# Two attentions with shared keys: a third bank for transposed score products, maxima turned on VectorE and sent through DRAM, values products at later steps

## The chip, the cores and the metric

The kernel runs on one core of one Trainium2 chip. The time is the device's, in microseconds (us), from the start to the end of one execution. Names: TensorE (PE; its weight loads PEld), VectorE (DVE), ScalarE (ACT), GpSimd (POOL), SyncE (SP, which issues DMAs here).

## The reference

A block of four layers on x of 4 x 512 x 512, each an attention and a feed-forward part. The change touches the attentions of layers 2 and 3, which compute the same thing (layer 3 names its arguments otherwise):

```python
def _L3_xattn_ref(q, k, v):
    QH, KVH = (32, 8)
    D = E // QH                      # 16
    G = QH // KVH                    # 4 query heads share one key head
    qh = q.reshape(b, s, KVH, G, D).transpose(0, 2, 3, 1, 4)
    kh = k.reshape(b, s, KVH, D).transpose(0, 2, 1, 3)
    vh = v.reshape(b, s, KVH, D).transpose(0, 2, 1, 3)
    scores = jnp.einsum('bkgsd,bktd->bkgst', qh, kh) * scale
    attn = jax.nn.softmax(scores, axis=-1)
    out = jnp.einsum('bkgst,bktd->bkgsd', attn, vh)
...
x = x + _L3_xattn_ref(_layernorm(x, axis=-1), ctx_512, ctx_512)
```

With a batch of 4 and 8 key heads there are 32 groups of four query heads in each layer, and 512 queries by 512 keys in each head.

## The kernel before

`stage_attend_shared` computes one such attention. Its unit of work is a *slot*: one group `s` of four heads (GROUPS is 32). Slots 1 to 24 are three turns of a loop over eight slots, the others are written out.

A group's scores are computed twice, in two forms. `scores` (L1529) puts queries on the partitions; 16 products of 128x512, two to a *set*. VectorE reduces each set to the maxima of its rows (`max_set`, L1648). Two buffers of two banks hold the sets (`score[m % 2]`), so the product of step 2m+4 waits until set m is reduced. `scores_T` (L1540) puts keys on the partitions, in 16 steps n (key tile n // 4, head n % 4), with the maximum already subtracted: the maxima of the group are two more rows of `qT` (high and low part), against rows of -1 in `kT`. ScalarE takes the exponential of each (L1628) into one of eight `probs`, and `results` (L1553, a round of four heads, after 4 of the 16 steps) multiplies them with the values into one bank `res`. The bank is copied out (`move_res`, L1620), turned on TensorE (`turn_results`, L1565), divided by its sum on VectorE (`finish`, L1663 and L1666) and added to x by GpSimd (L1701).

In slot s TensorE issues for each n the transposed product of group s and, right behind it, the plain product of group s + 2. The two read different halves of the partitions (`half(par, ...)`, bases 0 and 64, and the parities are opposite). After step LAST = 1 comes the last round of values products of the slot before, after steps 5, 9 and 13 (VALUES) the first three of this slot. After MAX = 5 comes `turn_max` (L1560): the split maxima of group s + 1 are turned by TensorE into bank 7, copied by ScalarE (`move_max`, L1615) and put into `qT` by four DMAs (`put_max`, L1495). After RES = 9 comes `turn_results` into the same bank 7. The transposed products alternate between two banks, 4 and 5, so that of step n waits for the exponential of step n - 2 (`exped`).

VectorE's slot has this order, which the change leaves as it is, and in which RES sets the place of `finish`:

```python
def slot(s, place, j, ahead):
    if ahead >= 1:
        split_maxima(s + 1, place + 1)
    for m in range(SETS):
        if ahead >= 2:
            max_set(s + 2, m)
        if m == (RES + 1) // 2 and not is_first(s):
            finish(s - 1)
```

SP loads group s + 3 in each slot (`load`, 12 DMAs, L1482 and L1485) and then puts the maxima of group s + 1. Before the first slot it also stores the queries' high and low parts to DRAM (`spill`, L1468), from which the loads read them.

Of the kernel before, what the change touches and what calls it, by code (L numbers as in the profile page):

```python
# [1384 lines left out]
def stage_attend_shared(k, nm, ctx_g, q_hi, q_lo, k_hi, k_lo, factor, queries):  # L1385
# [12 lines left out]
    LAST, VALUES, MAX, RES = 1, (5, 9, 13), 5, 9  # L1398
    with stage_room(k) as room:
        ctx, block = room.memory, room.block  # L1400

        def sb(name, shape, dt=F32):
# [14 lines left out]
        (cleared, consts, spilled, scored, maxed, max_split, turned_max, max_moved, scoredT, exped, valued, vals_kept, res_moved, turned_res,  # L1417
         inv_made, finished, added) = k.sems(
            ctx, nm, "cleared consts spilled scored maxed max_split turned_max max_moved scoredT exped valued vals_kept res_moved turned_res "
# [29 lines left out]

        @block.vector  # L1450
        def _(dve):
            for r in range(SLOTS):
                dve.memset(kT[r][:, :].bitcast(F32), -1.0).then_inc(cleared, 1)
            for r in range(2):
                dve.memset(vals[r][:, :, :], 0.0).then_inc(consts, 1)
                dve.memset(split[r][:, :, :, :].bitcast(F32), 0.0).then_inc(consts, 1)
            dve.wait_ge(consts, 4)
# [13 lines left out]
        def _(sp):  # L1471
# [15 lines left out]
            def put_max(place, j, g):  # L1487
# [15 lines left out]
            put_max(0, 0, 0)  # L1503
            sp.wait_ge(spilled, 2 * B * DMA)

            def slot(s, place, j, ahead):
                if ahead >= 3:
# [3 lines left out]
                if ahead >= 1:  # L1511
                    put_max(place + 1, j, s + 1)
# [4 lines left out]
        def _(pe):  # L1517
# [16 lines left out]
            def scores_T(g, place, j, n):  # L1534
# [4 lines left out]
                pe.wait_ge(exped, PAIRS * g + n + 1)  # L1539
                pe.matmul(scoreT[n % 2][:, :], kT[r][half(h % 2, USED + 2), t * P:(t + 1) * P], qT[r][half(h % 2, USED + 2), h // 2, :],  # L1540
# [15 lines left out]
            def turn_max(g, place):  # L1556

                pe.wait_ge(max_split, 2 * (g + 1))
# [1342 lines left out]
```

## Time and profile before

| | |
|---|---|
| median of 3 runs | 4062.18 us (4059.2 to 4066.68) |
| profiled execution, its time | 4080.94 us |
| its span | 4079.3 us |
| mean granted clock of TensorE | 0.91 of full |
| slots with all parts (1 to 29) | 29 in each of two layers |

The trace is of the one profiled execution. Durations and starts in it are in us from the span's start. A view gives for an instruction its start, its time, its engine and line, what it writes and reads, how many were merged (x4), and in brackets how long the engine was idle before it and which work released it. Matmuls overlap, so their times don't add up; their starts do. The granted clock is 1.00 at 2.4 GHz and 0.50 at 1.2 GHz.

### The profile page before, as it was taken

How to read it: one execution, taken by the hardware profiler on the slowest of the kernel's cores; microseconds unless marked ns; L12 is line 12 of the kernel's file. 1: busy time of each engine (PE TensorE's matmuls, PEld its weight loads, DVE VectorE, ACT ScalarE, POOL GpSimd, SP SyncE). 2: the span in 40 equal slices, each digit the busy share in tenths (PEclk: the TensorE clock that was granted, in tenths of full speed). 3: DMA queues.
4: the chain of work that ended last, by engine and by line, in shares of the span. 5: the costliest groups of instructions: out<-in, count | busy, mean ns of one | idle time of the engine just before them, and what ended most of it. 6: DMA issues, size and time to landing. Idle time of an engine off the chain costs nothing. (4 is left out here: it accounts for less than half of the span.)

```text
span 4079.3 us, 62234 instructions
## 1 busy us (share of the span) xinstructions
PE 3337.4 (82%) x17174; PEld 2276.6 (56%) x17174; DVE 2324.2 (57%) x3679; ACT 1934.3 (47%) x3331; POOL 606.2 (15%) x901
## 2 busy tenths in 40 slices
PE   3359996899871999668888689899897788878998
PEld 2137775666551788533332367888775233326886
DVE  6954445455443343477777444566567676745565
ACT  5643333355530555346666433566433566654333
POOL 2410001544223000210000030122111000000000
PEclk7669998999985999869999799999997999989999
DMA  3424442400011333341111152567443211102223
GB/s 137 147 98 139 139 138 89 165 0 0 11 52 62 111 119 107 111 152 43 42 41 32 70 183 93 193 242 240 167 141 119 71 40 41 42 21 67 96 94 113
DMA packets 174475, 404.47 MB, mean 99 GB/s; under 512 B 28484, under 2 KB 28612, under 8 KB 173682
## 3 DMA queue, kind: packets, MB, share of 16 engines
q1 hardware_dynamic: 141010, 286.47, 22.0%
q0 software_dynamic: 22480, 96.23, 6.9%
q10 hardware_dynamic: 10864, 20.45, 1.3%
q8 instruction: 41, 0.67, 0.1%
q14 instruction: 80, 0.66, 0.1%
HBM read 312.32 MB, written 87.03 MB: 98 GB/s over the span
## 5 line engine op out<-in xcount | busy, mean ns | idle before, releaser
L1648 DVE TENSOR_REDUCE at_maxima<-psum 128x2 f32<-128x1024 f32 x512 | 623.9, 1223 | 259.5 <-PE psum L1529 241.8
L1628 ACT ACTIVATE at_probs<-psum 128x512 f32<-128x512 f32 x1024 | 568.4, 595 | 368.0 <-PE psum L1540 337.6
L1540 PE MATMUL psum<-at_qT,at_kT 50*128 50x512 f32 x1024 | 452.1, 491 | 177.8 <-ACT at_probs L1628 167.7
L1540 PEld LDWEIGHTS psum<-at_qT,at_kT 50*128 50x128 f32 x1024 | 175.9, 192 | 496.9 <-ACT at_probs L1628 438.6
L1529 PE MATMUL psum<-at_kT,at_qT 48*128 48x512 f32 x1024 | 431.4, 496 | 14.6 <-DVE at_maxima L1648 12.4
L573 PE MATMUL psum<-f_xT_hi,ffn_w_hi 128*128 x1024 | 406.8, 397 | 9.9 <-DVE f_xT_lo L313 2.8
L573 PE MATMUL psum<-f_xT_lo,ffn_w_hi 128*128 x1024 | 405.9, 396 | 0.0
L1553 PE MATMUL psum<-at_probs,at_vals 128*32 128x512 f32 x2048 | 292.7, 640 | 0.0
L590 PE MATMUL psum<-ffn_w_hi,ffn_hid_hi 128*128 128x512 f32 x768 | 269.3, 391 | 1.3 <-ACT ffn_hid_hi L636 1.3
L387 PE MATMUL psum<-ident,n_normed 128*128 128x128 f32 x448 | 95.5, 389 | 195.9 <-ACT n_normed L353 159.3
L478 ACT ACTIVATE ffn_w_hi<-ffn_w_raw 128x512 fp32r<-128x512 f32 x262 | 161.6, 633 | 157.3 <-PE psum L595 100.1
L573 PEld LDWEIGHTS psum<-f_xT_hi,ffn_w_hi 128*128 128x128 f32 x1024 | 194.0, 189 | 56.7 <-issue 12.1
L486 DVE TENSOR_TENSOR ffn_w_lo<-ffn_w_raw,ffn_w_hi 128x512 fp32r<-128x512 f32 x262 | 176.7, 686 | 76.1 <-ACT ffn_w_hi L478 75.9
L573 PEld LDWEIGHTS psum<-f_xT_lo,ffn_w_hi 128*128 128x128 f32 x1024 | 193.9, 189 | 44.5
L595 PE MATMUL psum<-ffn_w_hi,ffn_hid_lo 128*128 128x512 f32 x768 | 205.3, 389 | 0.0
L1325 DVE TENSOR_REDUCE at_maxima<-psum 128x1 f32<-128x128 f32 (+3 forms) x256 | 122.5, 489 | 141.9 <-PE psum L1135 138.3
L573 PE MATMUL psum<-f_xT_hi,ffn_w_lo 128*128 x512 | 202.5, 396 | 0.0
L592 PE MATMUL psum<-ffn_w_lo,ffn_hid_hi 128*128 128x512 f32 x512 | 199.5, 390 | 0.0
L387 PEld LDWEIGHTS psum<-ident,n_normed 128*128 128x128 f32 x448 | 79.8, 204 | 212.0 <-issue 147.8
L1529 PEld LDWEIGHTS psum<-at_kT,at_qT 48*128 48x128 f32 x1024 | 170.8, 194 | 28.5 <-DVE at_maxima L1648 22.7
L676 DVE TENSOR_TENSOR n_normed<-n_normed,psum 128x512 f32<-128x512 f32 (+1 forms) x88 | 60.4, 687 | 217.2 <-ACT n_normed L633 211.0
L1296 ACT ACTIVATE at_probs<-psum 128x512 f32<-128x512 f32 (+3 forms) x256 | 111.9, 438 | 136.9 <-PE psum L1149 136.7
(399 smaller groups left out, 7354.9 us busy)
## 6 DMA issues: line engine op xcount, KB each, us to landing
ffn_w_raw<-in_stream SPq DMA_DIRECT2D x262, 256.0 KB, 2.7
ffn_w_hi<-quantized SPq DMA_DIRECT2D x66, 512.0 KB, 3.5
ffn_w_hi<-quantized SPq DMA_DIRECT2D x65, 256.0 KB
at_qT<-q_hi SPq DMA_DIRECT2D x256, 64.0 KB, 2.2
ffn2a_w_raw<-in_shared2a SPq DMA_DIRECT2D x26, 512.0 KB
ffn2b_w_raw<-in_shared2b SPq DMA_DIRECT2D x26, 512.0 KB
qz_raw<-in_stream SPq DMA_DIRECT2D x17, 768.0 KB, 4.2
quantized<-qz_quant POOLq DMA_DIRECT2D x16, 768.0 KB, 3.5
```

What stands on the lines that cost most here:

```text
L387: mm = pe.transpose(turned_ps[u][:, c, :], normed[u][:, c * P:(c + 1) * P], k.ident[:, :])
L478: act.activation(hi[slot][:, :], raw[slot][:, :], ACT.Copy).then_inc(made, 1)
L486: dve.tensor_tensor(lo[slot][:, :], raw[slot][:, :], hi[slot][:, :].bitcast(F32), ALU.subtract).then_inc(made, 1)
L573: mm = pe.matmul(hid_ps[h][s][0:n, :], wt[s][:, w], xt[:, c, bass.ds(b * S, S)], start=(c == 0 and i == 0), stop=(c == DC - 1 and i == len ...
L590: pe.matmul(out[t][:, :], hid_hi[s][0:n, tok], w2_hi[s][0:n, :], start=first, stop=False)
L592: pe.matmul(out[t][:, :], hid_hi[s][0:n, tok], w2_lo[s][0:n, :], start=False, stop=False)
L595: mm = pe.matmul(out[t][:, :], hid_lo[s][0:n, t * P:(t + 1) * P], w2_hi[s][0:n, :], start=False, stop=last)
L1529: mm = pe.matmul(score[m % 2][:, 512 * (n % 2):512 * (n % 2) + S], qT[r][half(par, USED), jj, t * P:(t + 1) * P], kT[r][half(par, USED), : ...
L1540: pe.matmul(scoreT[n % 2][:, :], kT[r][half(h % 2, USED + 2), t * P:(t + 1) * P], qT[r][half(h % 2, USED + 2), h // 2, :], start=True, sto ...
L1553: pe.matmul(res[h * OW:(h + 1) * OW, :], vals[place % 2][:, t, :], probs[n % RING][:, :], start=(t == 0), stop=(t == TB - 1), tile_positio ...
L1628: act.activation(probs[n % RING][:, :], scoreT[n % 2][:, :], ACT.Exp, scale=factor).then_inc(exped, 1)
L1648: dve.tensor_reduce(maxima[:, t, 2 * jj:2 * jj + 2], score[m % 2].rearrange("p (h s) -> p h s", h=2), AX.X, ALU.max).then_inc(maxed, 1)
```

## The change

1. Transposed score products rotate through three banks, 4 to 6 (`turn_of`); the results' bank moves to 7. The turned results no longer have a bank of their own: they take the place of one product in the rotation, after step RES, now 7. The transposed product of step n waits for the exponential of step n - 3 where the rotation allows, and that of step 10 waits for `finish` of the slot.
2. The maxima are no longer turned by TensorE and copied by ScalarE. VectorE splits them into a 128x32 tile, turns it by blocks of 32x32 (`across`), and SP sends that tile to a DRAM buffer `tops` (`send_max`, ahead of the loads) and reads it back into `qT` with four DMAs (`put_max`, behind the loads), whose pieces are 32 elements long.
3. LAST is 2 and VALUES are 6, 10, 14; `move_res` still follows the exponential of step 2.

`turn_max`, `move_max` and their waits go. `finish` keeps its rule, `m == (RES + 1) // 2`, so it follows set 4 where it followed set 5.

```diff
-    LAST, VALUES, MAX, RES = 1, (5, 9, 13), 5, 9
+    LAST, VALUES, MOVE, RES = 2, (6, 10, 14), 2, 7
+    TURNS = 3
...
-        maxima, inv = sb("maxima", [P, TB, H]), sb("inv", [P, TB, H])
-        split = [sb(f"split{r}", [P, TB, P // 2, 2], F32R) for r in range(2)]
-        maxT = [sb(f"maxT{r}", [2 * H, S]) for r in range(2)]
+        maxima, inv = sb("maxima", [P, H, TB]), sb("inv", [P, TB, H])
+        split = sb("split", [P, H, 2, TB], F32R)
+        across = [sb(f"across{r}", [P, 2 * H * TB]) for r in range(2)]
         result = sb("result", [P, TB, H * HD])
-        score, scoreT, res, turn = [room.psum[:, 1024 * m:1024 * m + 1024] for m in range(2)], room.banks[4:6], room.banks[6], room.tiles(7)
+        score, scoreT, res = [room.psum[:, 1024 * m:1024 * m + 1024] for m in range(2)], room.banks[4:4 + TURNS], room.banks[7]
+        turn = room.tiles(4 + (RES + 1) % TURNS)
...
+        def turn_of(n):
+
+            return (n if n <= RES else n + 1) % TURNS
...
+            def send_max(place, g):
+
+                sp.wait_ge(max_turned, g + 1)
+                sp.dma_start(tops[place % SLOTS, :, :], across[place % 2][:, :]).then_inc(max_out, DMA)
+
+            def put_max(place, g):
 
                 r = place % SLOTS
-                sp.wait_ge(max_moved, g + 1)
+                sp.wait_ge(max_out, DMA * (g + 1))
+                rows = tops[r, :, :].rearrange("(b h o t) i -> h o t b i", b=TB, h=H, o=2)
                 for jj in range(2):
                     for par in range(2):
                         at = HALF * par + USED
-                        row0 = 2 * (2 * jj + 1 - par)
-                        sp.dma_start(qT[r][at:at + 2, jj, :].bitcast(F32), maxT[place % 2][row0:row0 + 2, :]).then_inc(put[r], DMA)
+                        dst = qT[r][at:at + 2, jj, :].bitcast(F32).rearrange("o (t b i) -> o t b i", t=TB, b=TB)
+                        sp.dma_start(dst, rows[2 * jj + 1 - par]).then_inc(put[r], DMA)
 
             spill(sp, 0)
             sp.wait_ge(spilled, 2 * DMA)
@@ -1500,16 +1511,19 @@
                 load(g, 0)
             for b in range(1, B):
                 spill(sp, b)
-            put_max(0, 0, 0)
+            send_max(0, 0)
+            put_max(0, 0)
             sp.wait_ge(spilled, 2 * B * DMA)
 
             def slot(s, place, j, ahead):
+                if ahead >= 1:
+                    send_max(place + 1, s + 1)
                 if ahead >= 3:
                     if not is_first(s):
                         sp.wait_ge(scoredT, PAIRS * s)
                     load(place + 3, j)
                 if ahead >= 1:
-                    put_max(place + 1, j, s + 1)
+                    put_max(place + 1, s + 1)
...
-                pe.wait_ge(exped, PAIRS * g + n + 1)
-                pe.matmul(scoreT[n % 2][:, :], kT[r][half(h % 2, USED + 2), t * P:(t + 1) * P], qT[r][half(h % 2, USED + 2), h // 2, :],
+                if n < 2:
+                    pe.wait_ge(exped, PAIRS * g + n + 1)
+                elif n > 2:
+                    pe.wait_ge(exped, PAIRS * g + (n + 1 if RES < n < RES + TURNS else n))
+                if n == RES + TURNS and not is_first(g):
+                    pe.wait_ge(finished, g + 1)
+                pe.matmul(scoreT[turn_of(n)][:, :], kT[r][half(h % 2, USED + 2), t * P:(t + 1) * P], qT[r][half(h % 2, USED + 2), h // 2, :],
...
-            def turn_max(g, place):
-
-                pe.wait_ge(max_split, 2 * (g + 1))
-                for t in range(TB):
-                    mm = pe.transpose(turn[:, t, :], split[place % 2][:, t, :, :].rearrange("p c o -> p (c o)").bitcast(F32), k.ident[:, :])
-                mm.then_inc(turned_max, 1)
-
...
-                    if n == MAX and ahead >= 1:
-                        pe.wait_ge(max_moved, s + 1)
-                        if not first:
-                            pe.wait_ge(finished, s)
-                        turn_max(s + 1, place + 1)
                     if n == RES and not first:
                         pe.wait_ge(res_moved, s)
-                        if ahead >= 1:
-                            pe.wait_ge(max_moved, s + 2)
-                        else:
-                            pe.wait_ge(finished, s)
+                        pe.wait_ge(exped, PAIRS * s + n + 1)
                         turn_results()
 
             all_slots(pe, slot)
             results(GROUPS - 1, GROUPS - 1, TB - 1)
             pe.wait_ge(res_moved, GROUPS)
-            pe.wait_ge(finished, GROUPS)
             turn_results()
 
...
-            def move_max(g, place, j):
-
-                act.wait_ge(turned_max, g + 1)
-                if not (isinstance(g, int) and g < 2):
-                    act.wait_ge(put[(place + 2) % SLOTS], PUTS * DMA * (use(place - 2, j) + 1))
-                act.activation(maxT[place % 2][:, :], turn[0:2 * H, :, :].rearrange("p t q -> p (t q)"), ACT.Copy).then_inc(max_moved, 1)
...
-                    act.activation(probs[n % RING][:, :], scoreT[n % 2][:, :], ACT.Exp, scale=factor).then_inc(exped, 1)
-                    if n == LAST + 1 and not is_first(s):
+                    act.activation(probs[n % RING][:, :], scoreT[turn_of(n)][:, :], ACT.Exp, scale=factor).then_inc(exped, 1)
+                    if n == MOVE and not is_first(s):
                         move_res(s - 1)
-                    if n == MAX + 1 and ahead >= 1:
-                        move_max(s + 1, place + 1, j)
...
-                dve.tensor_reduce(maxima[:, t, 2 * jj:2 * jj + 2], score[m % 2].rearrange("p (h s) -> p h s", h=2), AX.X, ALU.max).then_inc(maxed, 1)
+                dve.tensor_reduce(maxima[:, 2 * jj:2 * jj + 2, t], score[m % 2].rearrange("p (h s) -> p h s", h=2), AX.X, ALU.max).then_inc(maxed, 1)
...
             def split_maxima(g, place):
-                hi, lo = split[place % 2][:, :, 0:H, 0], split[place % 2][:, :, 0:H, 1]
+                hi, lo = split[:, :, 0, :], split[:, :, 1, :]
                 dve.wait_ge(maxed, 2 + SETS * (g + 1))
-                if not (isinstance(g, int) and g < 2):
-                    dve.wait_ge(turned_max, g - 1)
+                if not (isinstance(g, int) and g < 1):
+                    dve.wait_ge(max_turned, g)
                 dve.tensor_copy(hi, maxima[:, :, :]).then_inc(max_split, 1)
                 dve.wait_ge(max_split, 2 * g + 1)
                 dve.tensor_tensor(lo, maxima[:, :, :], hi.bitcast(F32), ALU.subtract).then_inc(max_split, 1)
                 dve.wait_ge(max_split, 2 * g + 2)
+                if not (isinstance(g, int) and g < 2):
+                    dve.wait_ge(max_out, DMA * (g - 1))
+                dve.transpose(across[place % 2][:, :], split[:, :, :, :].rearrange("p h o t -> p (h o t)").bitcast(F32)).then_inc(max_turned, 1)
 
```

## Rows read from the trace of the kernel before

**Rows 1.** The page, busy us (share of the span) and instructions

```profile
PE 3337.4 (82%) x17174; PEld 2276.6 (56%) x17174; DVE 2324.2 (57%) x3679; ACT 1934.3 (47%) x3331; POOL 606.2 (15%) x901
```

**Rows 2.** Busy time by stretch, the last two slots of each stage

```profile
core 0: us, PE busy (x) PEld busy (x) DVE busy (x) ACT busy (x) POOL busy (x), PEclk, DMA share, GB/s
...
2240.12:2276.50 36.38, 29.99 (x120) 9.55 (x120) 2.48 (x7) 19.81 (x37) 1.68 (x3) 0.77 0.00 1
...
3618.30:3659.50 41.20, 34.61 (x120) 10.73 (x120) 2.88 (x9) 19.85 (x37) 1.68 (x3) 0.63 0.00 1
```

**Rows 3.** The same view, one slot (from split to split) a line

```profile
3215.39:3229.91 14.52, 11.96 (x74) 4.47 (x72) 10.65 (x13) 9.64 (x19) 0.97 (x2) 1.00 0.18 42
...
3456.55:3472.63 16.08, 13.51 (x74) 5.00 (x72) 10.64 (x13) 9.62 (x19) 0.96 (x2) 0.89 0.14 39
```

**Rows 4.** Timeline of TensorE in one slot: start, us, line, work, count [idle before <-releaser]

```profile
3218.59 0.50 PE L1540 MATMUL psum<-at_qT,at_kT 50*128 50x512 f32 x1 [0.40 <-ACT at_probs L1628]
...
3219.02 1.07 PE L1553 MATMUL psum<-at_probs,at_vals 128*32 128x512 f32 x8
...
3220.01 0.66 PE L1560 MATMUL psum<-ident,at_split 128*128 128x128 f32 x4
...
3220.60 0.50 PE L1540 MATMUL psum<-at_qT,at_kT 50*128 50x512 f32 x1
...
3220.60 0.72 PE L1529 MATMUL psum<-at_kT,at_qT 48*128 48x512 f32 x2
...
3220.94 0.39 PE L1540 MATMUL psum<-at_qT,at_kT 50*128 50x512 f32 x1
...
3221.78 0.49 PE L1540 MATMUL psum<-at_qT,at_kT 50*128 50x512 f32 x1 [0.46 <-ACT at_probs L1628]
```

**Rows 5.** Timeline of ScalarE and of VectorE in the same slot

```profile
3216.96 0.60 ACT L1628 ACTIVATE at_probs<-psum 128x512 f32<-128x512 f32 x1 [0.83 <-PE psum L1540]
...
3221.13 0.60 ACT L1628 ACTIVATE at_probs<-psum 128x512 f32<-128x512 f32 x1 [1.41 <-PE psum L1540]
...
3221.63 0.57 ACT L1615 ACTIVATE at_maxT<-psum 8x512 f32<-8x512 f32 x1
...
3215.60 0.18 DVE L1657 TENSOR_TENSOR at_split<-at_maxima,at_split 128x16 fp32r<-128x16 f32 x1
...
3219.16 1.22 DVE L1648 TENSOR_REDUCE at_maxima<-psum 128x2 f32<-128x1024 f32 x1 [0.70 <-PE psum L1529]
...
3225.55 1.23 DVE L1648 TENSOR_REDUCE at_maxima<-psum 128x2 f32<-128x1024 f32 x1 [1.02 <-PE psum L1529]
...
3226.69 0.25 DVE L1663 RECIPROCAL at_inv<-psum 128x16 f32<-128x16 f32 x1
...
3226.97 0.42 DVE L1666 TENSOR_TENSOR at_result<-psum,at_inv 128x256 f32<-128x256 f32 x1
```

**Rows 6.** Timeline of all engines, start of the second stage

```profile
3142.97 9.13 DVE L1648 TENSOR_REDUCE at_maxima<-psum 128x2 f32<-128x1024 f32 x8
...
3144.24 0.79 PE L1529 MATMUL psum<-at_kT,at_qT 48*128 48x512 f32 x2 [1.30 <-DVE at_maxima L1648]
```

**Rows 7.** SP's timeline in that slot, L1482 to landing, the second stage's first T

```profile
3214.25 0.34 SPq L1482 DMA_DIRECT2D at_qT<-q_hi  x1
...
3219.43 0.37 SPq L1485 DMA_DIRECT2D at_kT<-k_lo  x1
...
3222.22 2.44 SPq L1495 DMA_DIRECT2D at_qT<-at_maxT  x4
...
DMA to landing us min/median/max: 2.1/2.3/4.0
...
3170.56 0.79 PE L1540 MATMUL psum<-at_qT,at_kT 50*128 50x512 f32 x1 [9.78 <-DMA at_qT<-at_maxT]
```

**Rows 8.** Timeline of TensorE about one fall of the granted clock

```profile
3461.17 0.66 PE L1560 MATMUL psum<-ident,at_split 128*128 128x128 f32 x4
...
3463.88 0.49 PE L1540 MATMUL psum<-at_qT,at_kT 50*128 50x512 f32 x1 [0.37 <-ACT at_probs L1628]
...
3464.30 1.91 PE L1553 MATMUL psum<-at_probs,at_vals 128*32 128x512 f32 x8
```

More of the change, by code:

```diff
@@ L1382, in _, with stage_attend_shared @@
             finish(groups - 1)
-def stage_attend_shared(k, nm, ctx_g, q_hi, q_lo, k_hi, k_lo, factor, queries):
+def stage_attend_shared(k, nm, ctx_g, q_hi, q_lo, k_hi, k_lo, tops, factor, queries):
     HD, H, PARTS = HEAD2, 4, 3
@@ L1455, in _ @@
                 dve.memset(vals[r][:, :, :], 0.0).then_inc(consts, 1)
-                dve.memset(split[r][:, :, :, :].bitcast(F32), 0.0).then_inc(consts, 1)
-            dve.wait_ge(consts, 4)
+            dve.wait_ge(consts, 2)
             for r in range(2):
@@ L1485, in load @@
                         sp.dma_start(kT[r][at:at + HD, :].bitcast(F32), src[n * HD:(n + 1) * HD, tokens]).then_inc(landed[r], DMA)
-            def put_max(place, j, g):
+            def send_max(place, g):
+                sp.wait_ge(max_turned, g + 1)
+                sp.dma_start(tops[place % SLOTS, :, :], across[place % 2][:, :]).then_inc(max_out, DMA)
+            def put_max(place, g):
                 r = place % SLOTS
-                sp.wait_ge(max_moved, g + 1)
+                sp.wait_ge(max_out, DMA * (g + 1))
+                rows = tops[r, :, :].rearrange("(b h o t) i -> h o t b i", b=TB, h=H, o=2)
                 for jj in range(2):
@@ L1566, in turn_results @@
                 mm.then_inc(turned_res, 1)
-            pe.wait_ge(consts, 6)
+            pe.wait_ge(consts, 4)
             for g in range(2):
@@ L1571, in _ @@
                     scores(g, g, 0, n)
-                    if g == 1 and n == MAX:
+                    if g == 1 and n == 0:
                         pe.wait_ge(made, before + N // P)
-                        turn_max(0, 0)
             def slot(s, place, j, ahead):
@@ L1620, in move_res @@
                 act.activation(resT[:, :], res[:, :], ACT.Copy).then_inc(res_moved, 1)
-            move_max(0, 0, 0)
             def slot(s, place, j, ahead):
@@ L1642, in _ @@
             dve.sem_inc(finished, 1)
-            dve.wait_ge(consts, 6)
+            dve.wait_ge(consts, 4)
             def max_set(g, m):
@@ L1701, in add @@
                 pool.tensor_tensor(xt, xt, result[:, :, :], ALU.add).then_inc(added, 1)
-            pool.wait_ge(consts, 6)
+            pool.wait_ge(consts, 4)
             keep_values(0, 0)
@@ L2672, in build_program @@
         ("quantized", (D * 4 // P + 2, P, 3 * D)), ("gathered1", (N, D)), ("answers1", (N + 1, D)),
-        ("q_hi", (D, N)), ("q_lo", (D, N)), ("k_hi", (P, N)), ("k_lo", (P, N)), ("gathered2", ((BLOCKS2 + 1) * BLOCK2, D)), ("answers2", (BLOCKS2 * BLOCK2, D)))}
+        ("q_hi", (D, N)), ("q_lo", (D, N)), ("k_hi", (P, N)), ("k_lo", (P, N)), ("tops", (4, P, 32)), ("gathered2", ((BLOCKS2 + 1) * BLOCK2, D)), ("answers2", (BLOCKS2 * BLOCK2, D)))}
     with ExitStack() as program:
@@ L2777, in build_program @@
                 stage_attend_shared(k, f"at{layer}", ctx_g, scratch["q_hi"], scratch["q_lo"], scratch["k_hi"], scratch["k_lo"],
-                                    1.0 / np.sqrt(HEAD2), queries)
+                                    scratch["tops"], 1.0 / np.sqrt(HEAD2), queries)
                 with ExitStack() as q_ctx:
```

4 lines of the change are left out of this document (2 added, 2 removed).

## Prediction

> **What bounds the kernel now.** The page comes first: TensorE is busy in 82% of the span [rows 1], so a first thought would be that only its own work counts. The change touches only the two shared-key attentions, which end at 2276.5 and 3659.5 us [rows 2]. The view of busy time by stretch cuts them from one splitting of maxima to the next, which is one slot (one group of four heads). An undisturbed slot takes 14.51 or 14.52 us, and 49 of the 58 full slots lie within 0.11 us of that; two per layer hold a loop's jump, and five are about 1.5 us longer at a granted clock of 0.89 [rows 3]. In a slot TensorE is busy 11.96 us, VectorE 10.65, ScalarE 9.64: none is full, so what counts is who waits for whom.
>
> The timeline of one slot shows that [rows 4, 5]. I write T(n) for the transposed score product of step n (L1540), S(n) for the plain one (L1529), E(n) for its exponential, R(m) for the reduction of S(2m) and S(2m+1), V for a round of values products. T(n) and S(n) start together, and use different halves of the array's rows (bases 0 and 64, exchanged by parity). A V holds the engine 1.00 us (3219.02 to the turning at 3220.01), a turning 0.59 us; a lone pair holds it 0.43 us before a V may start (3218.59 to 3219.02), and a second pair starts 0.34 us after the first (3220.60, 3220.94) [rows 4]. ScalarE starts E 0.53 us after its T (3220.60 to 3221.13), its operations follow each other by 0.49, and the T that needs the bank starts 0.65 us after E started (3221.13 to 3221.78) [rows 4, 5]. With two banks for T that loop is what paces the slot: after each V ScalarE stood idle 0.83 us, after V and a turning 1.41 [rows 5]. VectorE is behind nobody: it starts R 0.57 us after a lone pair (3218.59 to 3219.16) or 0.46 after a second one, and every V stands behind an odd n, when the pair of products of a reduction is complete, so that R runs under the V.
>
> **The change, part by part.** All in us per slot, for a slot at full clock, counted from T(15) of the slot before, which now follows a V.
>
> *Removed:* the turning of maxima on TensorE (0.59) and the copy of maxT on ScalarE (0.57) [rows 4, 5]. ScalarE has slack, so only the first could matter.
>
> *Third bank:* T(n) needs E(n-3) and no longer E(n-2), save at n = 0, 1, 8, 9. It removes ScalarE's idle time behind each V. That is a real gain if nothing else waits.
>
> *Later V:* V now follows n = 2, 6, 10, 14, even steps, between S(2m) and S(2m+1). The reduction of that set can start only behind the V. S(2m+4) needs it (two score buffers), and S(2m+4) stands ahead of the next V in TensorE's order. So a stretch from V to V costs: 0.57 (S to the start of R), 1.27 from the start of R to the product that needs its buffer (3142.97 to 3144.24, the start of both stages, where VectorE paces) [rows 6], 0.43 for the last pair, 1.00 for V: **3.27**. TensorE's own work there is 1.00 + 0.43 + 3 x 0.23 = 2.12. (0.23: two pairs end 0.72 to 0.73 after their start, one 0.50 [rows 4].)
>
> *Turned results in the ring:* the turning now stands behind n = 7 and takes a ring bank, so T(10) waits for VectorE's finish of that slot. But VectorE's slot still has finish behind R(4), at (RES+1)//2 = 4, and R(4) needs S(9). That puts on TensorE's path what was hidden: S(9), R(4), reciprocal, multiplication, T(10). From row to row: R to reciprocal 1.14, to multiplication 0.28, its 0.42, 0.05 to the product: 1.89 (3225.55, 3226.69, 3226.97) [rows 5].
>
> The slot, worked through: T(15) 0; S(15) lets R(7) start at 0.57; S(2) waits for it, 0.57 + 1.27 = 1.84; V 2.27 to 3.27; S(3) 3.27, R(1) 3.84, S(6) 5.11, V 5.54 to 6.54; S(7) 6.54; turning 6.97 to 7.56; T(8) 7.56, T(9) 7.90; R(4) 7.90 + 0.46 = 8.36; T(10) 8.36 + 1.89 = 10.25; V 10.68 to 11.68; S(11) 11.68, R(5) 12.25, S(14) 13.52, V 13.95 to **14.95**. I checked that E never is late in it: the latest, E(3) behind the move of the results, starts at 3.87 and T(6) may start at 4.52, before S(6). So 14.95 for 14.51, **+0.44** a slot, though all the exponentials' waits are gone. The same rules give 14.51 for the old order (12 of its starts come out within 0.02), which is why I trust them to 0.3 (four latencies to 0.07 each). Over 2 x 29 slots that have all parts: **+25** (8 to 43).
>
> *VectorE's transpose* of 128x32: no row shows one. It stands between R(7) and R(0). Bound below by the 0.18 of the split's 128x16, above by the 0.42 of a 128x256 operation [rows 5]; I take 0.2. R(0) then starts at 2.53 and R(1) could at 3.67, before its 3.84: hidden up to 0.17 more; at the upper bound 0.05 a slot, 3 in all.
>
> *Maxima through DRAM:* one more DMA ahead of the 12 loads in SP's queue (each 0.37, about 0.47 apart, 3214.25 to 3219.80), then four puts in 2.44 and 2.3 to land [rows 7]. Split at 2.0, sent at about 2.5 to 3.0, loads to 8.6, puts to 11.05, landed 13.3; T(0) of the next slot is at 15.3. Hidden by 2.0. At the start of each stage it is not: the first T waits for the puts already (3170.56; 9.8 us of idle time), and now a send lands first, 2.3 + 0.4, behind the spills: I take 4 a layer, **+8** (4 to 12).
>
> *Tail:* slots 30 and 31 have no S, and take 36.4 and 41.2 us, much of it at half clock, TensorE busy 30.0 and 34.6 [rows 2]. There the third bank helps: 6.5 of idle time to about 2.5, a turning less: 5 a layer, **-10** (-14 to 0).
>
> *The clock.* The five falls inside ordinary slots came about the end of a stretch between V's that holds a turning and four pairs: in one of them a V had ended at 3461.17, TensorE then had two waits for ScalarE, the last of 0.37, and the next V, at 3464.30, took 1.91 for its 1.07 [rows 4, 8]. The gap without a V was 3.13. Each fall cost 1.4 to 1.6 (16.08 for 14.52 the longest) [rows 3]. In the changed slot V to V there is 4.14 long (6.54 to 10.68), one pair less, and TensorE idle for 2 us at T(10). With the shorter gap the clock fell in 5 of 58 slots; with a longer one and less work in it I expect it much more often. I take a fall in 7 of 10 slots (bounds: 5 of 58, and all), at 1.1 each, since part of the slow time falls on waiting (bounds 0.9 and 1.45): 58 x 0.7 x 1.1 = 45, less the 7 of before: **+38** (0 to 77). The Trainium skill ("TensorE: Matmul & The Clock Gate", part 1, on the clock gate) says that the half clock is the default and that activity releases it; by that rule the removed turning and the wait both speak against this change. The falls in this trace agree, as far as they go.
>
> **Sum:** 25 + 8 - 10 + 38 = +61. The profiled execution took 4080.9 (span 4079.3), so its like would take 4142; it lies 18.8 above the median of 4062.2. Against the median: **4123**.
>
> **Rivals.**
> *A, no more falls of the clock:* the order is as worked out, TensorE's wait costs no clock. For it: 53 of 58 slots hold their clock with a gap of 3.1 between V's. Against it: the new gap is a third longer. +23, so 4085. Chance 0.14.
> *B, faster:* finish is not on the path. If T(10) didn't wait beyond R(3) (7.11 + 1.27 = 8.38), the slot would be four stretches of 3.27 = 13.08, -1.43, 58 x -1.43 - 2 = -85: 3977. For it: ScalarE's idle waits of 0.83 and 1.41 do vanish. Against it: VectorE's order and rows 5. It decides only if the 1.89 chain came to under 1.4 a slot in all; at 1.45 the gain is zero. Chance 0.09.
> *C, the terms cancel:* latencies at their low ends (+8), no falls: within 8 us of before. Chance 0.07.
> *D, maxima late:* the puts read 128-byte pieces from DRAM. If they took three times their 2.44, they would land at 18.2, 2.9 behind T(0): 58 x 2.9 = 168 more than A: 4253. It bites from 4.4 of puts. For it: nothing in the rows. Chance 0.05. The Trainium skill ("DMA: Bandwidth & Descriptors", why small descriptors are slow) holds small pieces in HBM to be slow; the transfers here are too few bytes for bandwidth to decide, and no row shows their time.
> The forecast itself has 0.65.
>
> **The range.** Its own: 61 with the clock term from 10 to 77 and the slot term from 8 to 43 gives 4085 to 4165. To leave out no more than 2 in 10 I reach down over A and up a little: 4075 to 4172. A change of under 0.2% (8 us) can't be told from none here. Faster: B, 0.09. Same: C and a little of A, 0.08. Slower: 0.83.
>
> **What will show it.** Slots of about 14.95 at a granted clock of 1.00 and of 16 at about 0.9, most of them the latter; TensorE idle some 2 us in front of T(10), released by VectorE's multiplication; S(6) and S(14) released by R; no waits of 0.83 on ScalarE; POOL and SP free; the four puts landed before T(0). Wrong would make it: T(10) starting right behind T(9), S starts that don't wait for R, or a clock at 1.00 in slots of 14.95 (then A).

## The result and the profile after

The changed kernel took 4303.82 us (median of 4 runs, 4292.57 to 4315.3), the kernel before on the same chip 4060.69 us (4053.97 to 4066.68): a ratio of 1.0599, with a 95% interval of 1.0562 to 1.0637. The direction was forecast; the size was not. The time lies 181 us above the predicted 4123 and 132 us above the end of the range.

The profiled execution took 4315.3 us with a span of 4312.5, at a mean granted clock of 0.834 (before: 4080.9, 4079.3, 0.91). The page of the changed kernel, its line of busy times and the three largest groups:

```profile
PE 3586.3 (83%) x16914; PEld 2348.5 (54%) x16918; DVE 2323.3 (54%) x3739; ACT 1901.2 (44%) x3267; POOL 607.8 (14%) x901
...
L1639 DVE TENSOR_REDUCE at_maxima<-psum 128x2 f32<-128x1024 f32 x512 | 612.1, 1220 | 500.5 <-PE psum L1543 499.4
...
L1559 PE MATMUL psum<-at_qT,at_kT 50*128 50x512 f32 x1024 | 530.9, 621 | 167.2 <-DVE at_result L1660 120.3
...
L1572 PE MATMUL psum<-at_probs,at_vals 128*32 128x512 f32 x2048 | 414.6, 892 | 0.0
```

TensorE issues 260 instructions fewer than before and is busy 249 us more [rows 1]. That cannot be work; the same products became longer (T takes 621 ns in the mean, where the page of before has 491). And there is a new releaser of T (now L1559): VectorE's finish multiplication (L1660), with 120.3 us of idle time.

Busy time by stretch tells where. The first two lines are the 29 slots of each stage that have all parts (from the split of slot 2 to that of slot 31), the other two the slot that is followed below and the last full one:

```profile
core 0: us, PE busy (x) PEld busy (x) DVE busy (x) ACT busy (x) POOL busy (x), PEclk, DMA share, GB/s
1814.14:2363.15 549.01, 473.99 (x1973) 169.46 (x1970) 309.26 (x377) 264.97 (x493) 28.04 (x58) 0.68 0.13 32
3299.97:3852.84 552.87, 479.60 (x1973) 170.42 (x1970) 309.28 (x377) 264.88 (x493) 28.06 (x58) 0.68 0.13 32
2213.35:2230.32 16.97, 14.50 (x69) 5.50 (x68) 10.67 (x13) 8.96 (x17) 0.97 (x2) 0.79 0.14 37
3831.00:3852.84 21.84, 19.52 (x69) 6.50 (x66) 10.64 (x13) 9.20 (x17) 0.96 (x2) 0.50 0.01 2
```

The same 29 slots took 430.98 and 432.67 us before, at granted clocks of 0.98 and 0.97. They grew by 118.0 and 120.2, 238.2 together. A slot takes 18.93 and 19.06 us in the mean, from 16.8 (clock 0.80) to 21.95 (0.50); before, 14.52 at 1.00 and 16.08 at 0.89 [rows 3]. Not one of the 58 ran at the full clock throughout. VectorE's work per slot is as it was (10.67 for 10.65), ScalarE's is less, as the copy of the maxima is gone (8.96 for 9.64).

The rest of the difference: the first two slots of each stage grew by 4.7 and 5.5 (from the first split to the third: 25.17 and 34.32 before, 29.86 and 39.84 after); the last ones (from the last full split to the last copy of results) took 34.28 and 38.62 and take 36.29 and 36.30, so nothing in sum. In the starts, the stage's first T waited 3.58 us for the puts in the first stage, where it did not wait before, and 13.55 in the second, where it was 9.78 [rows 7]:

```profile
3281.92 0.79 PE L1559 MATMUL psum<-at_qT,at_kT 50*128 50x512 f32 x1 [13.55 <-DMA at_qT<-tops]
```

The stages are 248.1 us longer, the span 233.2: between the two stages, where no line was changed, this execution took 860.7 us and that of before 876.9.

TensorE's timeline of one slot of the changed kernel shows the new order (T(15) of the slot before at 2211.51). This slot began at the full clock:

```profile
2211.51 0.50 PE L1559 MATMUL psum<-at_qT,at_kT 50*128 50x512 f32 x1
...
2213.79 1.07 PE L1572 MATMUL psum<-at_probs,at_vals 128*32 128x512 f32 x8
...
2216.64 0.49 PE L1543 MATMUL psum<-at_kT,at_qT 48*128 48x512 f32 x1
2217.06 1.06 PE L1572 MATMUL psum<-at_probs,at_vals 128*32 128x512 f32 x8
...
2218.48 0.66 PE L1577 MATMUL psum<-ident,at_resT 128*128 128x128 f32 x4
...
2221.87 0.47 PE L1559 MATMUL psum<-at_qT,at_kT 50*128 50x512 f32 x1 [2.06 <-DVE at_result L1660]
2221.98 0.49 PE L1543 MATMUL psum<-at_kT,at_qT 48*128 48x512 f32 x1
2222.40 1.13 PE L1572 MATMUL psum<-at_probs,at_vals 128*32 128x512 f32 x8
...
2226.33 1.94 PE L1572 MATMUL psum<-at_probs,at_vals 128*32 128x512 f32 x8
...
2231.06 1.93 PE L1572 MATMUL psum<-at_probs,at_vals 128*32 128x512 f32 x8
...
2242.71 0.76 PE L1559 MATMUL psum<-at_qT,at_kT 50*128 50x512 f32 x1 [2.07 <-DVE at_result L1660]
...
2247.98 1.07 PE L1572 MATMUL psum<-at_probs,at_vals 128*32 128x512 f32 x8
```

Read the column of starts: from V to V 3.27 us, then, over the turning and the wait, 5.34. T(10) starts 10.36 after T(15), after 2.06 of idle time, released by the finish. The very next V is the last short one; then V's take 1.94 and stand 4.73 apart, until 2247.98. Between this T(10) and the pause in front of the next one TensorE stands idle 0.26 us in all. The granted clock in the same stretch, by 1 us:

```profile
2221.00:2222.00 1.00, 0.13 (x2) 0.16 (x2) 0.69 (x3) 0.00 (x0) 0.09 (x1) 1.00 0.13 36
2222.00:2223.00 1.00, 1.00 (x10) 0.31 (x10) 0.00 (x0) 0.60 (x1) 0.64 (x1) 1.00 0.03 5
2223.00:2224.00 1.00, 1.00 (x10) 0.50 (x4) 0.00 (x0) 0.00 (x0) 0.00 (x0) 0.64 0.05 8
...
2246.00:2247.00 1.00, 1.00 (x7) 0.45 (x3) 0.73 (x1) 0.76 (x2) 0.00 (x0) 0.50 0.00 0
2247.00:2248.00 1.00, 0.95 (x8) 0.38 (x6) 1.00 (x2) 1.00 (x3) 0.00 (x0) 0.92 0.00 0
```

The clock falls 1.4 us after the wait has ended, while the engine works again, to its lower level (0.50 of the granted clock is 1.2 GHz, 1.00 is 2.4), and stays there for 24 us, past the next slot's wait.

The trace's record of the granted clock can be counted over the 58 slots. A fall is the start of a stretch at half clock (a low stretch) in one of them; the mean length counts each to its end:

| | falls | half clock within the slots, us | mean length of a low stretch, us |
|---|---|---|---|
| before | 9 | 44 | 4.9 (3.4 to 10.2) |
| after | 41 | 703 | 18.8 (3.4 to 65) |

The two of 65 us begin in the last full slot of the first stage and the last but one of the second, and run on through the last slots; the other 39 have a mean of 16.5, the longest 37.6. All 41 begin 0.1 to 1.7 us after the finish of a slot has ended; T(10) starts 0.15 after it. The clock was full at the end of the finish in exactly these 41 slots, and in the other 17 it was already low: where the wait met a full clock, the clock was lost every time. The engine comes back either 3.9 to 4.6 us after a finish (24 times) or about 18 us after one, just ahead of the next wait (14 times).

VectorE's timeline of that slot, with the split, the new transpose and the chain to T(10):

```profile
2213.35 0.18 DVE L1646 CAST at_split<-at_maxima 128x16 fp32r<-128x16 f32 x1
...
2213.86 0.21 DVE L1652 STREAM_TRANSPOSE at_across<-at_split 128x32 f32<-128x32 f32 x1
2214.00 1.20 DVE L1639 TENSOR_REDUCE at_maxima<-psum 128x2 f32<-128x1024 f32 x1
...
2218.62 2.48 DVE L1639 TENSOR_REDUCE at_maxima<-psum 128x2 f32<-128x1024 f32 x2 [0.91 <-PE psum L1543]
2221.01 0.25 DVE L1657 RECIPROCAL at_inv<-psum 128x16 f32<-128x16 f32 x1
2221.30 0.42 DVE L1660 TENSOR_TENSOR at_result<-psum,at_inv 128x256 f32<-128x256 f32 x1
```

The two reductions from 2218.62 are R(3) and R(4). Only after R(4), in the order that RES sets, come the reciprocal and the multiplication, whose end at 2221.72 lets T(10) go.

SP's queue, in two lines of its timeline, the send of maxima to DRAM and the four puts:

```profile
2214.10 0.35 SPq L1495 DMA_DIRECT2D tops<-at_across  x1
...
2220.49 2.54 SPq L1506 DMA_DIRECT2D at_qT<-tops  x4
```

The four puts of 128-byte pieces are issued in 2.54 us, against 2.44 before [rows 7], and no T(0) waits for them in the full slots.

### The profile page after: what moved, and what is told of

Its sections match the earlier page's. It is cut to its first block and busy times, and to the rows that moved or that the text cites. A ratio compares the mean times of both kernels' runs of the same rounds, so it can differ in the third digit from the quotient of the medians.

```text
span 4312.5 us, 61624 instructions
## 1 busy us (share of the span) xinstructions
PE 3586.3 (83%) x16914; PEld 2348.5 (54%) x16918; DVE 2323.3 (54%) x3739; ACT 1901.2 (44%) x3267; POOL 607.8 (14%) x901
## 5 line engine op out<-in xcount | busy, mean ns | idle before, releaser
L1639 DVE TENSOR_REDUCE at_maxima<-psum 128x2 f32<-128x1024 f32 x512 | 612.1, 1220 | 500.5 <-PE psum L1543 499.4
L1621 ACT ACTIVATE at_probs<-psum 128x512 f32<-128x512 f32 x1024 | 549.3, 599 | 608.6 <-PE psum L1559 603.4
L1559 PE MATMUL psum<-at_qT,at_kT 50*128 50x512 f32 x1024 | 530.9, 621 | 167.2 <-DVE at_result L1660 120.3
L1559 PEld LDWEIGHTS psum<-at_qT,at_kT 50*128 50x128 f32 x1024 | 234.2, 262 | 675.7 <-issue 399.6
L1543 PE MATMUL psum<-at_kT,at_qT 48*128 48x512 f32 x1024 | 549.6, 635 | 18.4 <-DVE at_maxima L1639 14.7
L1572 PE MATMUL psum<-at_probs,at_vals 128*32 128x512 f32 x2048 | 414.6, 892 | 0.0
L573 PE MATMUL psum<-f_xT_hi,ffn_w_hi 128*128 x1024 | 405.8, 396 | 10.2 <-DVE ffn_w_lo L486 2.6
L1543 PEld LDWEIGHTS psum<-at_kT,at_qT 48*128 48x128 f32 x1024 | 231.1, 259 | 94.8 <-DVE at_maxima L1639 89.4
```

Source lines behind the costliest of these rows:

```text
L573: mm = pe.matmul(hid_ps[h][s][0:n, :], wt[s][:, w], xt[:, c, bass.ds(b * S, S)], start=(c == 0 and i == 0), stop=(c == DC - 1 and i == len ...
L1543: mm = pe.matmul(score[m % 2][:, 512 * (n % 2):512 * (n % 2) + S], qT[r][half(par, USED), jj, t * P:(t + 1) * P], kT[r][half(par, USED), : ...
L1559: pe.matmul(scoreT[turn_of(n)][:, :], kT[r][half(h % 2, USED + 2), t * P:(t + 1) * P], qT[r][half(h % 2, USED + 2), h // 2, :], start=True ...
L1572: pe.matmul(res[h * OW:(h + 1) * OW, :], vals[place % 2][:, t, :], probs[n % RING][:, :], start=(t == 0), stop=(t == TB - 1), tile_positio ...
L1621: act.activation(probs[n % RING][:, :], scoreT[turn_of(n)][:, :], ACT.Exp, scale=factor).then_inc(exped, 1)
L1639: dve.tensor_reduce(maxima[:, 2 * jj:2 * jj + 2, t], score[m % 2].rearrange("p (h s) -> p h s", h=2), AX.X, ALU.max).then_inc(maxed, 1)
```

## The experiments

Each kernel was timed against the kernel before on the same chip, and the kernel before took from 4060.69 to 4087.94 us in these comparisons, so ratios are compared and not times. "V" and the letters are those of the prediction.

| | V after steps | finish after | ratio to before (95%) | slot at full clock, us (worked out) | clock of the two stages |
|---|---|---|---|---|---|
| the change | 2, 6, 10, 14 | R(4) | 1.0599 (1.0562 to 1.0637) | none (14.95) | 0.68, 0.68 |
| filled wait | 2, 6, 10, 14 | R(4) | 1.0056 (1.0017 to 1.0095) | 15.02 (14.95) | 1.00, 0.93 |
| odd steps | 1, 5, 9, 13 | R(4) | 0.9815 (0.9795 to 0.9834) | 13.10 (13.0) | 0.95, 0.93 |
| early finish | 2, 6, 10, 14 | R(3) | 0.9890 (0.9859 to 0.9921) | 13.90 (13.7) | 0.96, 0.94 |
| both | 1, 5, 9, 13 | R(3) | 0.9576 (0.9552 to 0.9599) | 11.99 (12.0) | 0.99, 1.00 |

### The wait filled with products

If it is the pause in front of T(10) that costs the clock, work put into the pause must give it back; if the change's order or its memory traffic made the products long, more work can only add.

```diff
-    scores_T(s, place, j, n)
-    if ahead >= 2:
-        scores(s + 2, place + 2, j, n)
+    if n == RES + TURNS and not first and ahead >= 2:
+        for _ in range(9):
+            scores(s + 2, place + 2, j, n)
+        scores_T(s, place, j, n)
+    else:
+        scores_T(s, place, j, n)
+        if ahead >= 2:
+            scores(s + 2, place + 2, j, n)
```

S(10) is computed nine times instead of once, and ahead of T(10).

> The changed kernel, with step 10 of each full slot in another order: the plain product S(10) is issued nine times into its own buffer (start=True each time, so the value is the same) ahead of T(10), which waits for VectorE's finish. This adds eight products of 0.23 us each to the 2.06 us in which TensorE stood idle, and nothing to the path. Theory clock (the order itself costs 0.6 us a slot, all else is the granted clock, which falls because TensorE stands idle here): the granted clock stays at 1.00 in most slots, a slot takes 15.0 to 15.3 us, the whole kernel about 4061 + 58 x 0.6 + 7 = 4103 us, within 4090 to 4130. Theory order (the even places of V and the wait for finish cost the 4.1 us a slot themselves, the lower clock is only a consequence of more waiting that costs little): no faster than the changed kernel, 4300 or more, since work is added.

4104.2 us against 4086.64. The 29 slots of the two stages, by stretch, and TensorE's timeline about one T(10):

```profile
1812.38:2250.87 438.49, 405.48 (x2206) 172.91 (x2210) 309.36 (x378) 262.76 (x494) 28.05 (x58) 1.00 0.16 41
3194.03:3654.25 460.22, 429.32 (x2209) 181.62 (x2210) 309.36 (x378) 263.34 (x494) 28.05 (x58) 0.93 0.15 39
```

```profile
3401.44 2.83 PE L1543 MATMUL psum<-at_kT,at_qT 48*128 48x512 f32 x10
3403.90 0.47 PE L1559 MATMUL psum<-at_qT,at_kT 50*128 50x512 f32 x1
3404.30 1.06 PE L1572 MATMUL psum<-at_probs,at_vals 128*32 128x512 f32 x8
```

Some 235 products were added to each stage, and the ratio to the kernel before fell from 1.0599 to 1.0056, which is over 200 us. The pause is gone (2.83 us of products stand there), T(10) starts when it did, and the slot takes 15.02 at a granted clock of 1.00. The second stage has 0.93 because its first three full slots (22.73, 22.81 and 19.49 us) ran in a low stretch that had begun before them, 102 us long. Four falls are left. This shows both the cause of the low clock and, undisturbed, the cost of the change's order: 0.50 us a slot.

### Values products at odd steps, finish after R(3), and both

```diff
-    LAST, VALUES, MOVE, RES = 2, (6, 10, 14), 2, 7
+    LAST, VALUES, MOVE, RES = 1, (5, 9, 13), 2, 7
```

> The changed kernel with LAST = 1 and VALUES = 5, 9, 13 as before, so that a V stands behind a complete pair of products; the third bank, the maxima through DRAM and the wait for finish at T(10) stay. Theory clock: the reduction runs under the V again, V to V takes 2.1 to 2.6 us at most, the idle time before T(10) is 1.0 us and lies under no gap between V's as long as 4.1; the clock holds; worked out by the same rules a slot takes 13.0 us; 58 x -1.5 from before's 4061 and +7 at the starts: about 3980 us (3950 to 4030). Rival (the wait for finish alone brings the clock down, whatever the places of V): idle time before T(10) remains, clock about 0.7 in the stage, slots of 17 or more, 4180 us or more.

```diff
-                    if m == (RES + 1) // 2 and not is_first(s):
+                    if m == (RES - 1) // 2 and not is_first(s):
```

> The changed kernel with finish placed behind R(3) instead of R(4) in VectorE's order; the even places of V stay. Worked out by the same rules T(10) starts at 9.0 instead of 10.25 and a slot takes 13.7 us at full clock. Theory clock: the gap between V's falls from 4.1 to 2.9 us and the idle time from 2.06 to 0.9, the clock falls in some slots only: slots of 13.7 to 16, total 4020 to 4150. Rival (even places of V keep the clock down by themselves, by VectorE's pace): mean granted clock in the stage stays near 0.68 and the total above 4200.

> Both edits: V at odd steps 1, 5, 9, 13 and finish behind R(3). By the same rules T(10) no longer waits for finish (8.9 against 9.33) and a slot takes 12.0 us, close to the 10.9 us that VectorE needs; the clock holds. 58 x -2.5 + 7: about 3923 us (3900 to 3980), faster than before. Rival (the maxima's way through DRAM is too slow for a shorter slot: split at 2.0, sent 0.5 behind it, loads to 8.6, puts to 11.1, landed 13.4): T(0) of the next slot then waits for the puts, a slot takes about 12.9 us and the total is about 3975 with T(0) released by a DMA.

They took 4010.8, 4045.77 and 3914.32 us against 4086.64. The first stage of odd steps with a T(10) of its second stage, the first stage of early finish and the second of both:

```profile
1810.55:2206.64 396.09, 347.11 (x1972) 131.12 (x1970) 309.07 (x377) 259.76 (x494) 28.16 (x58) 0.95 0.17 45
```

```profile
3201.67 0.47 PE L1559 MATMUL psum<-at_qT,at_kT 50*128 50x512 f32 x1 [1.07 <-DVE at_result L1660]
```

```profile
1813.42:2229.41 415.99, 364.43 (x1977) 134.16 (x1978) 306.82 (x377) 263.27 (x494) 28.13 (x58) 0.96 0.17 43
```

```profile
3112.30:3464.99 352.69, 333.87 (x1972) 127.89 (x1970) 306.58 (x377) 259.87 (x494) 28.12 (x58) 1.00 0.20 50
```

Either edit turns the loss into a gain. With odd steps a V runs between R(4)'s products and T(10), and the idle time there is 1.07 instead of 2.06; 13 low stretches begin, 133 us in all. With the early finish the chain no longer holds R(4), and T(10) waits 0.80: 6 low stretches, 68 us. With both, TensorE is busy 333.87 of 352.69 us, one low stretch of 6.8 us begins, and the kernel is 172 us faster than the one before. The rival stated for it came true in small: in 13 of its 58 full slots T(0) waited 0.5 to 1.4 us for the puts out of DRAM, 10.9 us in all, so the maxima's way has no slack left in slots of 12 us. The count of products is within five in all three and in the change; only the order differs.

### The parts of the change alone

To see whether a part of the change is a loss by itself, two kernels. First the kernel before with the later values products alone:

```diff
-    LAST, VALUES, MAX, RES = 1, (5, 9, 13), 5, 9
+    LAST, VALUES, MAX, RES = 2, (6, 10, 14), 5, 9
```

> The kernel before with LAST = 2 and VALUES = 6, 10, 14 alone: two banks, maxima turned on TensorE, the copy of the results behind E(3). By the rules of the prediction V to V takes 3.27 where no turning lies between and 3.63 with one, 13.8 us a slot against 14.5, and the longest gap without a V is 2.6 us. Theory: later V's alone are no loss while finish is off TensorE's path; no falls of the clock, about 4061 - 58 x 0.7 = 4020 (4000 to 4060, against this call's run of before by its ratio 0.985 to 1.0). Rival (the even places bring the clock down by themselves): more than 4150, granted clock under 0.85 in the stage.

4063.96 us against 4087.94: 0.9942 (0.9921 to 0.9964), 13.83 a slot at the full clock (13.80 worked out). Then the changed kernel with the maxima's way through VectorE and DRAM kept and the rest as before (two banks for T, results in bank 6 and turned in bank 7 behind step 9, with the wait for the finish back ahead of that turning, V at odd steps):

```diff
-    LAST, VALUES, MOVE, RES = 2, (6, 10, 14), 2, 7
-    TURNS = 3
+    LAST, VALUES, MOVE, RES = 1, (5, 9, 13), 2, 9
+    TURNS = 2
...
-        turn = room.tiles(4 + (RES + 1) % TURNS)
+        turn = room.tiles(7)
...
-                if n == RES + TURNS and not is_first(g):
-                    pe.wait_ge(finished, g + 1)
```

> The kernel before with the maxima's new way alone: split, transposed on VectorE, sent to DRAM and read back; two banks, the turned results in a bank of their own behind n = 9, V at 5, 9, 13. The turning (0.59) goes, and E(7) no longer stands behind the copy of the maxima, so T(9) starts 0.45 earlier: 13.5 us a slot against 14.5. With +3.4 at each stage's start: 4061 - 58 x 1.0 + 7 = 4010 (3990 to 4050; ratio 0.982 to 0.995). Rival (the puts come late through DRAM): T(0) waits for a DMA in each slot, 4060 or more.

4032.28 us against 4087.94: 0.9862 (0.9826 to 0.9897), 13.46 a slot (13.5 worked out). The first stage of each:

```profile
1809.67:2220.42 410.75, 359.81 (x2087) 142.68 (x2086) 306.36 (x349) 283.21 (x523) 28.10 (x58) 0.98 0.16 42
```

```profile
1813.94:2216.70 402.76, 337.89 (x1972) 120.62 (x1970) 311.75 (x378) 266.72 (x494) 28.14 (x58) 0.96 0.17 44
```

Both parts are gains. What is left of the change is the turned results in the ring of T's banks, which puts the finish ahead of T(10). That is no loss by itself either: the kernel with odd steps has it too, with the finish still behind R(4), and stands at 0.9815. The loss needs two things together, the finish behind R(4) on TensorE's path and V's at even steps, which leave nothing to issue in the wait; taking away either one ends it.

### What ends a low stretch

The runs above show what brings the clock down, but not how long it stays down. A first idea was that the pauses at the reductions (S(2), S(6) and S(14) wait for R) keep the clock down. The changed kernel with T(2), T(6) and T(14) each computed three times:

```diff
-                pe.matmul(scoreT[turn_of(n)][:, :], ...).then_inc(scoredT, 1)
+                for again in range(3 if n in (LAST, VALUES[0], VALUES[2]) else 1):
+                    mm = pe.matmul(scoreT[turn_of(n)][:, :], ...)
+                mm.then_inc(scoredT, 1)
```

> The changed kernel, in which T(2), T(6) and T(14) are issued three times each into their own bank (start=True, only the last one signals), so that TensorE has products to issue while S(2), S(6) and S(14) wait for a reduction; nothing is done about the 2.06 us in front of T(10). Question: the clock stays low for 17 to 65 us at a time in the changed kernel. Theory 'return' (the wait at T(10) brings it down, the reductions' waits in each stretch from V to V keep it down): the clock still falls in nearly every slot but comes back within 3 to 7 us; slots of 16 to 17.5 us, total 4120 to 4210. Rival (low for so long because of the wait at T(10) alone): unchanged, 4280 or more. Second rival (more products anywhere hold the clock up): no falls, 4110.

4337.53 us against 4087.94: 1.0628 (1.0562 to 1.0693). Some 175 more products ran in the full slots of each stage; the first stage:

```profile
1815.83:2381.81 565.98, 492.34 (x2149) 194.14 (x2146) 309.35 (x377) 273.90 (x494) 28.14 (x58) 0.69 0.13 31
```

There were 46 low stretches of 14.1 us in the mean, and 666 us at half clock within the slots against 703. The slots took 1116.65 us against 1101.88. The clock did not come back, and that idea fell; the first rival, written down as 4280 or more, is what was seen. It also shows that the products of the filled wait helped by their place: six more a slot elsewhere gave nothing.

The other question was the length of the pause. The kernel with odd steps was given a later finish, by reciprocals into spare tiles ahead of its own, five and then fifteen of them (`range(5)`, `range(15)`):

```diff
+                for i in range(15):
+                    dve.reciprocal(spare[i][:, :, :], r[:, :, :, HD])
                 dve.reciprocal(inv[:, :, :], r[:, :, :, HD]).then_inc(inv_made, 1)
```

> The kernel with V at odd steps (e1_odd), in which VectorE's finish is made about 1.1 us longer by five more reciprocals of the turned results into tiles that nothing reads. TensorE then waits about 2 us in front of T(10), as in the changed kernel, but the stretches from V to V hold no wait for a reduction. At full clock a slot takes about 14.2 us. Theory (the wait at T(10) makes the clock fall, and where it stays low for 19 us a fall it is because of the even places of V): it falls in most slots here too, but comes back after 3 to 10 us; slots of 15 to 16.5, total 4090 to 4170. Rival (how long it stays low depends on the wait at T(10) alone): falls last 17 us and more, clock about 0.7 in the stage, slots of 18 and a total of 4240 or more.

> As e8_odd_late, with fifteen added reciprocals (0.11 us each in that trace) for five: TensorE waits about 2.7 us in front of T(10), and the gap between the V's about it is 4.4 us, as long as the changed kernel's 4.3, with four pairs of products in it; V stands at odd steps. About 14.75 us a slot at full clock. Theory 'gap' (what brings the clock down is a gap of over 4 us between V's with the wait in it; what keeps it down for 19 us at a time is that the stretches with V at even steps have their products spread out by waits for reductions): falls in most of the 58 slots, each back within 3 to 10 us, slots of 16 to 17, total 4130 to 4200. Rival (low for as long as in the changed kernel wherever V stands): slots of 18.5 and more, clock near 0.7, total 4280. Second rival (V at odd steps holds the clock in any case): no more than the ten falls of e8_odd_late, 4110.

Five gave 4043.55 us against 4080.45: 0.9908 (0.9876 to 0.9940), 13.64 a slot. Both expectations missed: the five took 0.69 together and not 1.1, so the wait did not reach 2 us, and the falls that the theory asked for in most slots did not come. Fifteen gave 4253.65 against 4077.52: 1.0448 (1.0415 to 1.0481), with falls in every slot as the theory had it, but above its 4130 to 4200 and below the rival's 4280: the mean slot took 17.6 us where 16 to 17 was said. TensorE's timeline about one T(10), of five and of fifteen:

```profile
3310.32 1.07 PE L1573 MATMUL psum<-at_probs,at_vals 128*32 128x512 f32 x8
...
3313.01 0.47 PE L1560 MATMUL psum<-at_qT,at_kT 50*128 50x512 f32 x1 [1.63 <-DVE at_result L1663]
...
3314.60 1.10 PE L1573 MATMUL psum<-at_probs,at_vals 128*32 128x512 f32 x8
```

```profile
3400.71 1.06 PE L1573 MATMUL psum<-at_probs,at_vals 128*32 128x512 f32 x8
...
3404.51 0.47 PE L1560 MATMUL psum<-at_qT,at_kT 50*128 50x512 f32 x1 [2.74 <-DVE at_result L1663]
...
3406.11 1.72 PE L1573 MATMUL psum<-at_probs,at_vals 128*32 128x512 f32 x8
```

| | idle before T(10), us | V to V over it, start to start less the 1.00 of a V, us | falls in 58 slots | mean low stretch, us (without those that run on past the full slots) |
|---|---|---|---|---|
| odd steps | 1.07 | 2.7 | 13 | 10.2 (7.7) |
| with 5 more | 1.63 | 3.28 | 8 | 7.7 (7.7) |
| with 15 more | 2.74 | 4.40 | 58 | 9.4 (8.8) |
| the change | 2.06 | 4.34 | 41 | 18.8 (16.5) |

So in slots with V at odd steps a pause of 1.63 us does not cost the clock: its 8 falls all lie in the two slots a stage that hold a loop's jump and the two behind the second of them, and slots with a jump hold falls in kernels without the pause too. One of 2.74 costs it in every slot. But the count does not simply rise with the pause: at 1.07 us there were 13 falls, each 1.8 to 2.4 us after a finish, and none of them in a slot with a jump or the one behind it. The slot's own length differs as well (13.10, 13.64, and 14.75 worked out), and no run separates it from the length of the pause. And at such a gap as the change's the low stretches are half as long with V at odd steps. How long the clock stays down is thus not set by the pause alone.

Where it was lost, half-clock time has one price. The time over the full-clock slot, divided by the time at half clock within the slots, is 231 / 703 = 0.33 in the change, 168 / 505 = 0.33 with fifteen reciprocals (against the 14.75 worked out), and 31 / 97 = 0.32 with odd steps (against 13.18, the mean of its 34 slots at full clock).

## Why the prediction was right in direction and wrong in size

**The order at the full clock: right.** The start times worked out for the slot, counted from T(15), against those of the slot shown: V 2.27 and 2.28, V 5.54 and 5.55, turning 6.97 and 6.97, T(8) 7.56 and 7.56, T(9) 7.90 and 7.90, T(10) 10.25 and 10.36, V 10.68 and 10.89. The slot of 14.95 is seen in the filled-wait kernel: 15.02. So the term was 0.50 x 58 = 29 us, where 25 was said. The same working gave 13.0, 13.7, 12.0, 13.80 and 13.5 for kernels that measured 13.10, 13.90, 11.99, 13.83 and 13.46.

**The wait for the finish: right**, 2.06 us where 2 was said, in front of T(10), released by the multiplication. **Rival B** (faster, finish not on the path; 13.08 a slot, 85 us gained) therefore fell. The early finish comes nearest to it, with 13.90 a slot and 41 us gained, for T(10) still waits 0.80 there.

**The clock: the step that failed.** "I take a fall in 7 of 10 slots, at 1.1 each" has two factors. The first came out, 41 falls in 58 slots, but that was luck: it was meant as a chance for each slot, and the clock fell in every slot that still had it, 41 of 41; the other 17 had not got it back. The second took each fall to be as short as those inside ordinary slots of the kernel before: they were 3.4 us at half clock, so 1.1 was 0.32 us lost per us. The price per us held (0.33). The length did not: 18.8 us in the mean. The term is the mean slot over the full-clock one, 19.00 - 15.02 = 3.98, less the 14.89 - 14.52 = 0.37 of before, times 58: **+209 us, where +38 was said and 77 was the upper bound**. That bound took one fall a slot as the worst, as if a fall could not outlast its slot; the one shown above reaches past the next slot's wait. The slots forecast, most of 16 us at a clock of 0.9, were from 16.8 at 0.80 to 21.95 at 0.50. The five falls that the prediction went by were ones that the kernel recovered from at once [rows 8], and their length belongs to that kernel's order. The old trace held a sign of this that was left out: the four slots with a loop's jump each had a fall as well, of 3.4 to 10.2 us, and the slot with the longest took 19.16 for 14.51 (a part of it may be the jump's own):

```profile
3422.87:3442.03 19.16, 16.34 (x74) 6.00 (x72) 10.65 (x12) 10.02 (x19) 0.97 (x2) 0.73 0.11 32
```

**Rival A** (no more falls) and **rival C** (terms cancel, no falls) fell with it.

**The starts: right**, +10 where +8 was said; of these, 3.6 and 3.8 are the first T's longer waits for the puts. **The tail: wrong**, 0 where -10 was said; the last slots now run at half clock throughout (0.50, where it was 0.75 and 0.60), in the low stretches of 65 us that began in the full slots, so the lost clock is there too against the gain of the third bank, which no run shows alone. **The transpose: right**, 0.21 where 0.2 was taken, hidden. **Maxima through DRAM: right**, hidden in the full slots; rival D fell, with puts of 2.54 us where it needed 4.4. **ScalarE's waits: wrong as put.** ScalarE did not stop waiting for T: it stood idle 603.4 us for it, 337.6 before, and in the slot shown 1.03 us behind a V (to 2218.58). What went is TensorE's side of that loop: in the full slots TensorE waited 25.0 us for exponentials where it had waited 153.0, and 119.6 for the finish instead.

In sum, by measured terms: 29 + 209 + 10 + 0 = 248 us in the stages, where 61 was said. The medians differ by 243. The wait's length, its place and the loss of the clock at it were foreseen; what failed is the time that the clock stays lost.

**What stays open:** why a low stretch ends when it does. The ends gather at two places in the slot, one right behind the V and the undisturbed pairs after T(10). The products added elsewhere did not help, and V at odd steps shortened the stretches; no run tells what in those orders does it. Long ones occur without the pause too: 31 us with later V's alone and 34 us with the maxima's way alone, both from a slot with a loop's jump on, and the 102 us of the filled wait from the start of a stage.

## What to carry to other kernels

When a buffer is moved into a rotation that TensorE reuses, write down which engine must have read it and what stands ahead of that read in that engine's order: here the finish was free as long as its bank was its own, and its place in VectorE's order (behind R(4)), with V's at even steps, made it a pause of 2 us a slot. Price such a pause in a busy slot at what it can do to TensorE's clock and not at its length, and when a fall is priced, take its length as unknown up to several slots, since the falls in the old trace show only how fast the old order recovers. A cheap probe tells the two costs apart: fill the pause with products whose result is thrown away, and look at the slot.

## What the runs showed of the hardware that was not expected

TensorE can stay at half clock while the profile shows it busy: from 2223.46 to 2240.20 us, ahead of the next wait, it was busy 16.48 of 16.74 us at a granted clock of 0.50. Single low stretches lasted up to 65 us in the change and 102 with the filled wait. Adding some 470 products to the kernel took its ratio from 1.0599 to 1.0056, since they kept the clock.

The step from harmless to harmful is narrow: with V at odd steps a pause of 1.63 us a slot left 8 falls in 58 slots, one of 2.74 us made 58, and with V at even steps one of 2.06 us was enough each time that the clock was full.
